# Another opening and count loop with unread TensorE products, and the lower half of h's last tile behind the fourth adjacency tile

## The reference

```python
h = x @ W + b
adj = zeros((N, N)); adj[row, col] = 1; adj[col, row] = 1
adj = adj + eye(N)
adj = adj / maximum(adj.sum(axis=1, keepdims=True), 1)
out = w[0] * h
cur = h
for i in range(3):
    cur = adj @ cur
    out = out + w[i + 1] * cur
return relu(out)
```

## Time and profile before

| | |
|---|---|
| median of 3 runs | 394.41 us (390.25 to 394.6) |
| the profiled execution | 394.55 us, span 392.7 us |
| PE busy | 375.0 us (95%) |
| DVE, ACT, POOL busy | 283.7, 237.3, 103.3 us |
| mean granted clock of PE | 0.974 |

### The profile page before, as it was taken

One profiled execution on the slowest core, in us unless ns is written; L12 is line 12 of the kernel. 1 busy time (PEld: TensorE's weight loads), 2 busy tenths in 40 slices (PEclk: granted clock), 3 DMA queues, 4 the chain that ended last, 5 costly groups with the idle time before them and its releaser, 6 DMA issues.

```text
span 392.7 us, 7713 instructions
## 1 busy us (share of the span) xinstructions
PE 375.0 (95%) x2721; PEld 221.2 (56%) x2721; DVE 283.7 (72%) x603; ACT 237.3 (60%) x405; POOL 103.3 (26%) x95
## 2 busy tenths in 40 slices
PE   6899989999999999999999999999999999999980
PEld 2445557544444444444444444444558889999980
DVE  8899997629995776115765554554795979999994
ACT  9999965493922255302562111367876999999225
POOL 5102000059730167400693000177400000111120
PEclk9999985999999999999999999999999999999996
DMA  5960060006000000000253000034203112210005
GB/s 169 385 212 1 0 216 2 1 6 209 3 0 0 0 0 3 1 2 0 45 102 68 0 0 2 1 80 83 53 3 112 55 53 93 72 55 4 3 3 216
DMA packets 27974, 22.70 MB, mean 58 GB/s; under 512 B 19552, under 2 KB 20768, under 8 KB 27936
## 3 DMA queue, kind: packets, MB, share of 16 engines
q1 hardware_dynamic: 27072, 19.06, 16.9%
q10 hardware_dynamic: 864, 3.15, 2.1%
HBM read 15.87 MB, written 2.13 MB: 46 GB/s over the span
## 4 chain that ended last, share of the span: by engine, by line
PE 86%; DVE 9%; issue 2%; ACT 1%; DVEq 0%; ACTq 0%; POOL 0%; POOLq 0%
PE ps L772 22%; PE ps L1168 9%; PE ps L1109 7%; PE ps L1010 7%; PE ps L1051 7%; PE ps L964 7%; PE ps L973 7%; PE ps L819 7%; PE ps L939 4%; PE ps L954 4%; PE ps L840 3%; DVE cts L1610 1%; PE ps L890 1%; PE ps L858 1%; DVE c L1311 1%
## 5 line engine op out<-in xcount | busy, mean ns | idle before, releaser
L772 PE MATMUL ps<-big,xTs 128*128 128x512 f16 x384 | 84.3, 379 | 0.0
L772 PEld LDWEIGHTS ps<-big,xTs 128*128 128x128 f16 (+1 forms) x384 | 37.0, 98 | 43.4
L687 ACT ACTIVATE big<-big,uvt 128x1024 bf16<-128x1024 f32 x55 | 58.8, 1149 | 0.0
L588 ACT ACTIVATE big<-xcur,nmr,rstd (+1 forms) x24 | 19.5, 813 | 33.5 <-DVE nmr L1441 33.5
L442 POOL TENSOR_TENSOR big<-xcur,big x16 | 18.5, 1154 | 60.5 <-ACT xcur L589 59.8
L819 PE MATMUL ps<-big,xTs 128*128 128x512 f32 x64 | 32.2, 603 | 0.0
L459 POOL TENSOR_TENSOR xcur<-xcur,c 128x512 f32<-128x512 f32 (+2 forms) x8 | 8.8, 1105 | 88.3 <-DVE c L1644 86.3
L412 POOL TENSOR_TENSOR big<-xTs,big 128x2048 f16<-128x2048 f32 x4 | 16.2, 4080 | 53.7 <-ACT big L481 53.7
L1109 PE MATMUL ps<-big,cst 128*128 128x260 f16 x256 | 29.8, 275 | 0.0
L481 ACT ACTIVATE big<-ps 128x512 f16<-128x512 f32 (+2 forms) x17 | 9.6, 565 | 31.7 <-PE ps L772 30.9
L1010 PE MATMUL ps<-cst,big 128*128 128x512 f16 x128 | 27.8, 379 | 0.6 <-issue 0.6
(11 more groups left out here) (220 smaller groups left out, 712.8 us busy)
## 6 DMA issues: line engine op xcount, KB each, us to landing
big<-u_rows ACTq DMA_DIRECT2D x6, 512.0 KB, 3.8
xcur<-in_x SPq DMA_DIRECT2D x1, 2048.0 KB, 17.0
out<-xcur SPq DMA_DIRECT2D x8, 256.0 KB, 2.3
big<-in_W SPq DMA_DIRECT2D x1, 1024.0 KB, 6.1
xTs<-in_xT SPq DMA_DIRECT2D x1, 1024.0 KB, 10.2
big<-in_W3T SPq DMA_DIRECT2D x1, 1024.0 KB, 12.1
xTs<-in_W1T SPq DMA_DIRECT2D x1, 1024.0 KB, 5.5
xTs<-in_wc SPq DMA_DIRECT2D x1, 1024.0 KB, 8.0
```

The source lines that it names most:

```text
L687: act.activation(above[:, a % AHEAD, :], uf[:, h % 2], ACT.Relu, scale=BIG, bias=vb[:, j, h:h + 1]).then_inc(S["above_in"], 1)
L772: return mm(bank, lhs(k)[a], rhs(k)[b], start=start and k == 0 and n == 0, stop=stop and k == KT - 1 and n == 2)
```

## The change

- **Opening, DVE and ACT.** The test for edges outside the window is one product (`f_off`, relative position times its distance beyond the window, both counted from 1) instead of two comparisons; a key outside becomes 0. The small integer steps for the first columns stand ahead of the one-hots. ACT zeroes its part of c32 in three pieces and casts f_lo between the first two; the third stands behind its first squares. POOL keeps only constants and zeroing; DVE makes f_cell and f_far behind quads 2 and 3. PE's semaphore increments at its start go to POOL.
- **Count loop.** H_TO 29 instead of 27, and the number of h parts in a quad grows with q. LO_TURN 16 instead of 8: DVE makes the low one-hots of 15 quads instead of 13. WARM changes. In `add_window` the wait for the product comes first and the one for the previous addition is in the instruction. Banks of h and of the transposed blocks change.
- **Unread products.** `fill(n)`: n products of 256 columns into an unused half of bank 2, three behind each window from quad 29, five behind each of the first three left casts, four ahead of the branch.
- **Behind the loop.** The third transposed block no longer waits for the first evacuation; blocks 4 to 7 wait for one evacuation more. h_lower of the last tile stands behind the fourth adjacency tile; PE waits for it only at the last tile of the outer phase. The flag of the branch is loaded ahead of the last two windows.

```diff
-H_TO = 27
-LO_TURN = 8
-WARM = (8, 1, 4, 2)
+H_TO = 29
+LO_TURN = 16
+WARM = (8, 2, 4, 1)
+FILL_FROM, FILL = 29, (3, 5, 4)
+LOW_AFTER = 3
...
-                return NT * KT * (i - H_FROM) // (H_TO - H_FROM)
+                return NT * KT * sum(37 + j for j in range(H_FROM, i)) // sum(37 + j for j in range(H_FROM, H_TO))
...
-            part = c32[:, 0:ZERO_ACT, :].rearrange("p a n -> p (a n)")
-            copy(part, zero[:].broadcast_to([P, ZERO_ACT * N])).then_inc(S["c32z"], 1)
...
+            zeros(0, F_LO_AFTER)
+            act.wait_ge(S["prep"], LO_IN)
+            copy(f_lo, i_lo).then_inc(S["f_lo_in"], 1)
+            zeros(F_LO_AFTER, 2 * F_LO_AFTER)
...
             distances(0)
+            zeros(2 * F_LO_AFTER, ZERO_ACT)
...
+            def fill(n):
+
+                for _ in range(n):
+                    mm(ps[:, 2, HALF // 2:HALF], iota_lo[:], cur[:, 0, 0, 0, 0:HALF // 2],
+                       start=True, stop=True)
+
...
                     ins.then_inc(S["win_done"], 1)
+                    if q >= FILL_FROM:
+                        fill(FILL[0])
...
-            pe.wait_ge(S["cst_left"], NT // 2)
+            for n in range(NT // 2):
+                pe.wait_ge(S["cst_left"], n + 1)
+                if n < NT // 2 - 1:
+                    fill(FILL[1])
...
             attention_columns(2)
-            pe.wait_ge(S["cts_ready"], 1)
-            ct_block(2).then_inc(S["ct_done"], 1)
             attention_columns(3)
             pe.wait_ge(S["win_free"], NG)
+            ct_block(2).then_inc(S["ct_done"], 1)
             ct_block(3).then_inc(S["ct_done"], 1)
+            fill(FILL[2])
...
-            pe.wait_ge(S["h_lo"], NT)
             pe.wait_ge(S["cts_ready"], 2)
             for j in range(NT):
                 pe.wait_ge(S["adj_ready"], j + 1)
+                if j == NT - 1:
+                    pe.wait_ge(S["h_lo"], NT)
...
-                    if j >= 1:
-                        pe.wait_ge(S["cts_ready"], j + 2)
+                    pe.wait_ge(S["cts_ready"], j + 3)
...
-                if w:
-                    dve.wait_ge(S["win_free"], w)
+                dve.wait_ge(S["win_done"], w + 1)
...
-                added._wait_ge(S["win_done"], w + 1)
+                if w:
+                    added._wait_ge(S["win_free"], w)
...
                 if t == 0:
                     cast_right(2)
+                if t == LOW_AFTER:
                     for n in range(tiles_low, NT):
                         h_lower(n)
```

More of the change, by code:

```diff
@@ L77 @@
 FAR_QUAD = 5
-BASE_IN, LO_IN, HI_IN, REL_IN, NEG_IN, PLACE_IN, BAD_IN, F_KEY_IN = range(4, 12)
+BASE_IN, LO_IN, REL_IN, HI_IN, OFF_IN, PLACE_IN, F_KEY_IN = range(5, 12)
 BIG = 2.0 ** 40
@@ L189, in build @@
         e_dst, e_src, i_hi, i_lo = (tmpi[:, i, :] for i in range(4))
-        f_rel, f_neg, f_bad, f_lo, f_place, f_key, f_cell, f_far = (tmp[:, i, :] for i in range(4, 12))
+        f_rel, f_off, f_bad, f_lo, f_place, f_key, f_cell, f_far = (tmp[:, i, :] for i in range(4, 12))
         row_i = sb("row_i", [NG, 2], I32)
@@ L391, in _ @@
             pool.memset(c32[:, ZERO_ACT:ZERO_POOL, :], 0.0).then_inc(S["c32z"], 1)
+            pool.wait_ge(S["win_done"], 2)
+            pool.sem_inc(S["p_free"], 2)
+            pool.sem_inc(S["back_done"], 2)
+            for name, n in (("p_ready", 2), ("back_free", 1), ("z_lo", 2), ("alpha_in", 2), ("uc_in", 2), ("left_t", 1), ("y_lo", 2),
+                            ("exp_in", 4), ("most_free", 1)):
+                pool.sem_inc(S[name], n)
             pool.memset(abT[:], 0.0).then_inc(S["const_ready"], 1)
@@ L495, in _ @@
             act.wait_ge(S["tr"], 1)
-            copy(lo16[:], by_chunk(ps[:, 2, 0:E // P])).then_inc(S["nslo_in"], 1)
+            act.activation(lo16[:], by_chunk(ps[:, 2, 0:E // P]), ACT.Copy, bias=1.0).then_inc(S["nslo_in"], 1)
             copy(nslo[:], by_chunk(ps[:, 2, 0:E // P]), -1.0).then_inc(S["nslo_in"], 1)
@@ L539, in _ @@
                     act.wait_ge(S["tr"], 3)
-                    copy(far, by_chunk(ps[:, 5, 0:E // P])).then_inc(S["far_in"], 1)
+                    act.activation(far, by_chunk(ps[:, 5, 0:E // P]), ACT.Copy, bias=-1.0).then_inc(S["far_in"], 1)
                 if tiles_up < NT and h_quad(tiles_up) + 3 <= q:
@@ L871, in _ @@
             for q in range(NQ):
+                if q == FILL_FROM:
+                    pe.wait_ge(S["acc0"], 1)
+                    pe.wait_ge(S["h_lo"], 1)
                 quad(q)
@@ L1339, in _ @@
             key_hots(2, 0)
-            dve.wait_ge(S["c32z"], 3)
-            dve.wait_ge(S["first_in"], 8)
+            dve.wait_ge(S["c32z"], 5)
             tiles_low = 0
-            first = first_columns(0)
             key_hots(2, 1)
@@ L1353, in _ @@
                     lo_hots(q + LOOK)
-                elif tiles_low < NT and h_quad(tiles_low) + (4 if q < NQ - 2 else 3) <= q:
+                elif tiles_low < NT - 1 and h_quad(tiles_low) + (4 if q < NQ - 2 else 3) <= q:
                     h_lower(tiles_low)
                     tiles_low += 1
+                if q == FAR_QUAD - 3:
+                    stt(f_cell, i_hi, float(N), e_dst, ALU.mult, ALU.add).then_inc(S["far_a"], 1)
+                if q == FAR_QUAD - 2:
+                    dve.wait_ge(S["far_a"], 1)
+                    stt(f_far, f_cell, 1.0, f_bad, ALU.add, ALU.mult).then_inc(S["idx_far"], 1)
                 if q == FAR_QUAD + 2:
@@ L1371, in _ @@
             cast_right(0)
-            dve.wait_ge(S["far_in"], 2)
-            with dve.If(flag(dve, 0)):
+            with dve.If(far_seen):
                 dve.wait_ge(S["cst_dve"], 1)
```

90 lines of the change are left out of this document (42 added, 48 removed).

## The result

The changed kernel takes 395.28 us (median of 19 runs, 393.49 to 396.42), the kernel before, on the same chips, 391.19 (19 runs, 390.21 to 395.96). The ratio is 1.0093, 95% interval 1.0072 to 1.0114: the change makes the kernel 0.9% slower. By the 2% bound that is "same"; against the forecast (389.7, range 387.0 to 393.0) it is a miss, by size and by sign.

What follows compares the result with a forecast made beforehand. DVE sets the count loop's end, then PE, at half clock, is the bound. Starting the step 3.0 us earlier and running it at full clock (1.8) takes 4.8 from 394.55: 389.7 us, range 387.0 to 393.0.

Steps and rivals of the forecast that it cites:

- Count loop, PE.: PE in the count loop: h parts keep their cost, reach quad 28, and h is done at 52.7.
- the clock falls as before: Rival, chance 0.07: PE's clock falls about 55 despite unread products, the last part starts 3.1 later; put at 397 us.
- The opening: Before the count loop: first addition near 10.0, 0.8 earlier, bounds 0 and 1.2.
- the rival with a chance of 0.08: The opening gives nothing: clock falls near 11 or ACT's zeroing delays; 0.8 lost, perhaps another 0.8; 391 us.
- The loop's end: DVE's count loop, 49.1 long before, becomes 48.7 and ends at 58.7, bounds 57.5 and 60.6.
- The rival of the early loop: Chance 0.09: all DVE idle time goes, the loop ends at 57.5, the step starts 1.2 earlier; 388.5 or 387 us.
- The unread products: Around the loop's end on PE: they hold the clock at 1.00 from 50 to 80, at 0.11 us each.
- rival in which it falls behind 50: Clock falls late, at the step (chance 0.18, 391.6 us), or about 55 as before (0.07, 397 us).
- the fifteen at the casts: Unread products at the left casts: they end at 58.0, just behind the last cast; cost bounds 0.2 and 1.6.
- The step: First diffusion step on PE: 15.7 us at full clock instead of 17.5; the moved subtraction costs nothing there.
- The rule on transposes: Transposes and narrow columns ahead of the step look idle, so the clock falls at its first products; 391.6 us.
- The reference point: Gain of 4.8 us set against one profiled execution of 394.55; a run of 390.25 kept only as scatter warning.

Runs made afterwards that it cites:

- before_late_bank: The kernel before with one wait added: the first part of h's seventh tile waits for five lower halves instead of four; 394.08 us.
- rotated: The changed kernel with h's tiles using banks 2, 3, 4, 5 in turn; attention columns and first unread product wait for five lower halves; 389.48 us.
- old_banks: The changed kernel with the banks of h and transposed blocks as before and h_lower of the last tile made in the loop again; 389.91 us.
- thin_fill: The rotated kernel with its 37 unread products cut from 256 to 8 columns; 387.93 us.
- before_again: The kernel before, unchanged, run again for a second profile; 391.07 us.
- pad_ahead: The rotated kernel with 37 unread products of 8 columns, all ahead of the branch, none behind windows or at casts; 393.42 us.
- thin_again: The same kernel as thin_fill, repeated; 388.20 us.
- thin_few: The rotated kernel with 10 unread products of 8 columns in place of 37 of 256; 388.01 us.
- rotated_no_fill: The rotated kernel without any unread product; 392.99 us.

## Why the prediction was wrong, step by step

**The step that failed** is "*Count loop, PE.* The h parts cost what they did (32 of 0.86)". It took the bank change for bookkeeping, although the order on both engines gives the wait without any trace. From the code, of change and of before, with `h_parts` and the rule by which DVE takes up h_lower:

| | first part of tile 6 | waits for h_lower of | which DVE makes behind |
|---|---|---|---|
| before | quad 21 | tile 3 | quad 18 |
| changed | quad 24 | tile 4 | quad 24 |
| before_late_bank | quad 21 | tile 4 | quad 21 |

PE had finished quad 24 when DVE began the additions of quad 23; a wait with no quad between takes that lead away, 3.6 us here, and the idle PE then lost its clock. The arithmetic of the 5.86 between changed and rotated: 3.62 idle, 3.46 - 1.72 = 1.74 for two h parts at half clock, and 0.44 already lost ahead of it (quad 23's first addition starts at 42.34, in rotated at 41.90). Sum 5.80. The runs bear it out from both sides: without the wait the kernel takes 389.5 (rotated) and 389.9 (old_banks), and the kernel before with it 394.1. None of my rivals had this wait; "the clock falls as before" had the right sign by another mechanism, in a place where the clock held.

**The opening**: it gave more than its sum, and its rival came as well. The first addition starts at 9.53 (forecast 10.0, before 10.79), so it gives 1.3 and not 0.8, beyond its bound of 1.2. But in this profile the clock fell behind the opening (windows of all engines; PE's busy time is the first number behind the length, the clock the one ahead of the last two):

```profile
12.00:14.00 2.00, 2.00 (x7) 0.73 (x7) 1.67 (x9) 1.97 (x6) 0.00 (x0) 0.50 1.05 385
14.00:16.00 2.00, 2.00 (x12) 0.98 (x9) 1.73 (x9) 2.00 (x6) 0.00 (x0) 0.77 1.05 387
```

It falls to half between 10 and 16 in six of the nine profiles with the new opening and stays at 1.00 in three (rotated, old_banks, thin_fill). In the six, quad 23's first addition starts at 42.2 to 42.4, in the three at 41.9 to 42.0: the fall costs 0.2 to 0.5, and the 0.44 above is this price. So the rival with a chance of 0.08 was the commoner case in its mechanism; "perhaps another 0.8" was too much. With the old opening the clock fell there in one profile of five (before_late_bank).

**The loop's end**: not seen in the changed kernel (its cast starts at 62.41). In rotated it is at 56.67, forecast 58.7: DVE was quicker than my sum by 2.0, of which 0.45 is the opening. Of the rest 1.0 is a term that I put at nothing: the 59 one-hots of the keys together took 22.1 us instead of 22.7, the 64 additions 22.8 instead of 23.2, why is open. And h was done at 50.8 (forecast 52.7), early enough for the casts to end at 55.75, forecast 57.8. At quad 23 the changed kernel was 2.2 us ahead of before (42.34 against 44.58) just before it stalled. The rival of the early loop was the truer one here, and it brought nothing, because PE came next.

**The unread products**: the clock held, as forecast, and no rival in which it falls behind 50 occurred. But in the sum the fifteen at the casts were at their bound of 0.2 (the casts end at 57.8, they at 58.0). With casts done at 55.75 they cost their full 1.6. The two errors cancel in the main: rotated's transposes start at 57.70, forecast 58.0; its step at 61.81, forecast 62.0; its last part at 77.57, forecast 77.7; its time 389.44, forecast 389.7. **So the time forecast fits the kernel without the bank wait, but partly by luck: the loop's end was 2.0 us too late in the sum and the fifteen products 1.4 too cheap.** The gain that it stood for does not fit, as the reference point shows.

**The step**: 15.76 in the changed kernel (67.67 to 83.43), forecast 15.7. The moved subtraction at 71.72 leaves no gap of PE. Right.

**The rule on transposes** gave 391.6, and its mechanism did not occur: in the changed kernel and in rotated the transposes and 40-column products ahead of the step run at 1.00 throughout, and the step begins at full clock. In before_again the clock even rose within 60 to 61, when since 58.42 only transposes and 40-column products had run. The Trainium skill, "TensorE: Matmul & The Clock Gate", Part 4 (PE-mode transpose), says that transposes do not count as busy in the same way; these traces don't show it, although pad_ahead, where the clock came back only in the step, at 69, would fit it.

**The reference point.** I set 4.8 us against one execution of 394.55. 1.8 of them were the step at full clock, but in the commoner execution of the kernel before the clock is back in time, and its step lasts 79.05 - 63.28 = 15.8 already. By their ratios to the kernel before (0.9944 and 0.9911) rotated gains 0.6% and thin_again 0.9%, not the 1.2% of my sum; against the last part of before_again rotated gains 1.5 us and not 4.8. The run of 390.25, which I left as scatter, was the typical one.

**Open**: why the clock comes back after 6.8 us in one profile of the kernel before and after 13.6 in the other; what the stall at 147 hangs on; what the three slower runs of thin_few and the one of thin_fill are; why the clock holds in some executions of the new opening.

## What to carry to other kernels

A table of buffers is a table of waits: for each reuse, write down behind which work the reader frees the buffer and ahead of which work the writer needs it, in steps of the loop, before anything is said of time. If the difference is smaller than the lead that the writer has, it costs that lead, and on PE the clock as well. Price a change against several executions, for a clock that falls in a gap returns at different times; and when idle time is filled with unread products, try the narrowest, at the gap itself: here 8 columns did what 256 did, for some 1.5 us less, but only in the kernel whose real work left small gaps.

## What the runs showed that was not expected

- The same kernel has half clock for 6.8 us in one execution and 13.6 in another, which makes 3.4 to 3.9 us of 391.
- With products of 8 columns behind the windows and at the casts of the rotated kernel the clock stayed at 1.00, although PE was busy for only 1.33 of the 2 us from 54 to 56 (thin_fill; 1.19 in thin_few). Without any it was busy for 0.65 of them, and the clock fell to 0.50 within 58 to 59 (rotated_no_fill).
- A fall of the clock in the first 16 us, in six of nine profiles of the new opening, moves all that follows by 0.2 to 0.5 us: as much as some of the differences that one profile of each kernel was meant to show.
- Behind a branch PE can wait 2.33 us for "issue" in the middle of a row of products, in one of fourteen profiles; in the others 0.7 together at most.
